# A fused attention, linear-attention and mixture-of-experts kernel: one written-out order for every engine, and a first block table after five of eight images

## What is computed

```python
# 1. attention inside each image, with a key mask, added to x
sim = softmax(q.T @ k / sqrt(64) + key_mask);  x = x + gamma * (sim @ v)
# 2. on tokens t (8 images x 256 pixels, 128 channels), with LayerNorm: causal
#    linear attention of 8 heads over the IMAGE axis: image i sums over images 0..i
t = t + linear_attention(layer_norm(t)) @ out_w.T + out_b
# 3. with LayerNorm: 8 experts, the top 2 of each token, weights normalised
h = silu(x @ w1[e]) * (x @ w3[e]);  t = t + sum over the 2 chosen e of weight * (h @ w2[e])
```

## Time and profile before

| | |
|---|---|
| time, median of 3 runs (lowest to highest) | 201.02 us (199.63 to 201.24) |
| profiled execution, its own time | 201.14 us |
| its span, first to last instruction | 199.3 us |
| PE busy, share of the span | 147.9 us, 74% |
| DVE, POOL, ACT busy | 126.2, 88.2, 73.5 us |
| DMA moved | 16.91 MB |

### The profile page before, as it was taken

One profiled execution on the slowest core, in us unless ns is written; L12 is line 12 of the kernel. 1 busy time (PEld: TensorE's weight loads), 2 busy tenths in 40 slices (PEclk: granted clock), 3 DMA queues, 4 the chain that ended last, 5 costly groups with the idle time before them and its releaser, 6 DMA issues.

```text
span 199.3 us, 4128 instructions
## 1 busy us (share of the span) xinstructions
PE 147.9 (74%) x1125; PEld 129.2 (65%) x1125; DVE 126.2 (63%) x464; ACT 73.5 (37%) x222; POOL 88.2 (44%) x94
## 2 busy tenths in 40 slices
PE   0879999999979589684943057999999999992000
PEld 0557788798767457383823045999999999991000
DVE  2526776799989595997365500667767676752263
ACT  2357686667362204221114001444444444440000
POOL 0001111022023718087787750278787878776000
PEclk9999999999999967996555555999999999999555
DMA  5889600000000101011111714223243333110595
GB/s 131 228 265 363 247 3 0 0 3 0 0 5 13 40 0 56 1 43 42 40 57 53 153 48 105 62 79 92 76 100 84 92 92 85 47 53 0 178 251 204
DMA packets 15476, 16.91 MB, mean 85 GB/s; under 512 B 3083, under 2 KB 14032, under 8 KB 15198
## 3 DMA queue, kind: packets, MB, share of 16 engines
q1 hardware_dynamic: 12606, 12.14, 20.8%
q0 software_dynamic: 2272, 4.24, 6.8%
q10 hardware_dynamic: 576, 0.27, 0.8%
HBM read 10.76 MB, written 6.33 MB: 86 GB/s over the span
## 4 chain that ended last, share of the span: by engine, by line
PE 54%; issue 11%; DVE 11%; DMA 8%; POOL 7%; SPq 3%; ACT 3%; POOLq 0%; DVEq 0%; ACTq 0%
PE ps L759 18%; PE ps L768 8%; POOL rows_x L449 4%; PE ps L610 3%; DMA y<-rows_y 3%; PE ps L630 3%; PE ps L750 2%; PE ps L669 2%; PE ps L690 2%; PE ps L595 2%; DVE num L920 2%; DMA XT<-in_x_tok 2%; PE ps L596 2%; PE ps L620 2%; DVE xrow L952 2%
## 5 line engine op out<-in xcount | busy, mean ns | idle before, releaser
L461 POOL DMA_INDIRECT rows_y<-yb,xb x39 | 43.9, 1124 | 21.9 <-DVE yb L1068 21.0
L759 PE MATMUL ps<-xbT,WB 128*128 128x128 f32 x312 | 42.7, 282 | 0.0
L449 POOL DMA_INDIRECT rows_x<-xrow,slot x32 | 32.3, 1008 | 22.8 <-DVE slot L1013 14.2
L759 PEld LDWEIGHTS ps<-xbT,WB 128*128 128x128 f32 x312 | 39.4, 198 | 0.1
L433 POOL TENSOR_TENSOR rs<-ve,CF 128x2 f32<-128x2 f32 x8 | 5.6, 702 | 42.9 <-DVE ve L863 42.9
L1068 DVE TENSOR_SCALAR yb<-ps,xb 128x128 f32<-128x128 f32 x39 | 13.7, 351 | 17.2 <-PE ps L768 17.2
L572 ACT ACTIVATE gate<-ps 128x256 f32<-128x256 f32 x39 | 14.9, 383 | 25.6 <-PE ps L759 25.6
L768 PE MATMUL ps<-W,hid 128*128 x156 | 23.7, 276 | 0.5 <-DVE hid L1051 0.5
L1051 DVE TENSOR_TENSOR hid<-gate,ps 128x256 f32<-128x256 f32 x39 | 16.0, 411 | 11.0 <-ACT gate L572 11.0
L768 PEld LDWEIGHTS ps<-W,hid 128*128 128x128 f32 x156 | 20.5, 192 | 0.7 <-issue 0.7
L566 ACT ACTIVATE xbT<-ps 128x128 f32<-128x128 f32 x39 | 10.8, 277 | 19.3 <-PE ps L750 19.3
(11 more groups left out here) (126 smaller groups left out, 281.2 us busy)
## 6 DMA issues: line engine op xcount, KB each, us to landing
xb<-rows_x SPq DMA_DIRECT2D x39, 65.0 KB, 2.0
W<-in_w SPq DMA_DIRECT2D x1, 2048.0 KB, 10.3
y<-rows_y SPq DMA_DIRECT2D x8, 192.0 KB, 4.8
X<-in_x_ch SPq DMA_DIRECT2D x8, 128.0 KB, 2.9
XT<-in_x_tok SPq DMA_DIRECT2D x8, 128.0 KB, 3.4
W<-in_w SPq DMA_DIRECT2D x1, 1024.0 KB, 12.4
out_tok<-y SPq DMA_DIRECT2D x4, 192.0 KB, 3.6
rows_y<-yb,xb POOLq DMA_INDIRECT x39, 2.4
```

Source lines behind the costliest of these rows:

```text
L449: pool.indirect_dma_start(rows_x, bass.IndirectOffsetOnAxis(ap=slot[:, g:g + 1], axis=0), xrow[:, i * T + t, c, :], None, bounds_check=DUM ...
L461: pool.indirect_dma_start(rows_y, bass.IndirectOffsetOnAxis(ap=xb[:, n, DEST_COL:ROW].bitcast(I32), axis=0), yb[:, n, :], None, bounds_che ...
L759: last = pe.matmul(ps_gu[s % 3][:, k * P:(k + 1) * P], WB[:, s % WBS, k * P:(k + 1) * P], xbT[:, s % XBT, :], start=True, stop=True)
```

## The change

The steps and lags go. Each engine's list is written out call by call, and so is the PSUM bank of every call (thirteen tables of numbers; any of the eight banks can serve any purpose). In the written lists, stages one and two overlap:

- **Two tables.** `TABLES` holds (images counted, blocks, first block). After five images a first table hands out 13 blocks, only whole ones of 128 rows (the count is rounded down); after eight a second one hands out the other 26, starting where the first left off (`table_taken`), rounded up.
- **The first 13 blocks' w1 and w3** come from DRAM by a DMA on SP each (`load_weights`, 256 KB); the other 26 are copied by DVE as before.
- **Normalisations on ACT.** `lin_norm` and `route_norm` become activations with scale and bias. POOL prepares them: the eps addition comes from DVE, and -mean and -mean*rstd are new, so `rstd_lin` and `rstd_ffn` are four POOL instructions in place of one, with two waits on POOL's own semaphore.
- **Weighting on ACT**: `weigh` is an activation with a per-row scale. The silu table is loaded in mid-stage (`silu_set`).
- The 16 extra matmuls ahead of stage two (`WARM_MATMULS`) go. All eight pads are issued by SP, and five constants by ACT's queue. The first image's x and its token copy have semaphores of their own. y1 and y2 reuse the space of XT and X. Buffers grow: XBT, GATE, HID, WBS from 4, 3, 4, 3 to 6, 4, 5, 5.

```diff
-XBT, GATE, HID, WBS = 4, 3, 4, 3
-BANKS_XBT, BANKS_GU, BANKS_YB = (0, 1), (3, 4, 6), (2, 5)
+XBT, GATE, HID, WBS = 6, 4, 5, 5
+TABLES = ((5, 13, 0), (8, 26, 13),)
+BANK_CQK = (1, 3, 5, 0, 7, 2, 2, 6)
...
-WARM_MATMULS = 16
-STEPS = B + 12
...
             def rstd_ffn(i):
-                pool.wait_ge(ve2_done, i + 1)
+                b = i % 2
+                pool.wait_ge(mv2_done, 2 * (i + 1))
                 if i >= 2:
                     pool.wait_ge(xrow_done, 2 * (i - 1))
-                pool.tensor_tensor(rs2[:, i % 2, :], ve2[:, i % 2, :], CF[:, C_HALF:C_HALF + T], ALU.pow).then_inc(rs2_done, 1)
+                pool.tensor_scalar(nm2[:, b, :], mv2[:, b, :, 0], -1.0, None, ALU.mult)
+                link(pool.tensor_scalar(ve2[:, b, :], mv2[:, b, :, 1], LN_EPS, None, ALU.add))
+                link(pool.tensor_tensor(rs2[:, b, :], ve2[:, b, :], CF[:, C_HALF:C_HALF + T], ALU.pow))
+                pool.tensor_tensor(nb2[:, b, :], nm2[:, b, :], rs2[:, b, :], ALU.mult).then_inc(rs2_done, 1)
...
+            def route_norm(i):
+                b = i % 2
+                act.wait_ge(rs2_done, i + 1)
+                for t in range(T):
+                    act.activation(xrow[:, i * T + t, :, 0:P], t2[:, i * T + t, :].unsqueeze(1).broadcast_to([P, TOP_K, P]),
+                                   ACT.Identity, bias=nb2[:, b, t:t + 1], scale=rs2[:, b, t:t + 1]).then_inc(xrow_done, 1)
...
+            for k, (_, blocks, first) in enumerate(TABLES):
+                if k == len(TABLES) - 1:
+                    pad_lists()
+                sp.wait_ge(table_done, k + 1)
+                for n in range(k + 1):
+                    images = TABLES[n][0] - (TABLES[n - 1][0] if n else 0)
+                    sp.wait_ge(scattered[n], 16 * images * T * TOP_K)
+                if k == len(TABLES) - 1:
+                    sp.wait_ge(pads_stored, 16 * (E + 1))
+                for s in range(first, first + blocks):
+                    load_rows(s)
+                    if k < len(TABLES) - 1:
+                        load_weights(s)
...
+            def weigh(s):
+                n = s % RING
+                act.wait_ge(yb_done_pe, s + 1)
+                if s >= RING:
+                    act.wait_ge(yb_stored[n], 16 * (s // RING))
+                act.activation(yb[:, n, :], bank(BANK_YB[s])[:, 0:P], ACT.Copy, scale=xb[:, n, W_COL:W_COL + 1]).then_inc(yb_done, 1)
...
+            rstd_lin(0); rstd_lin(1); rstd_lin(2); rstd_lin(3); rstd_ffn(0); rstd_lin(4); rstd_ffn(1)
+            scatter(0, 0); scatter(0, 1); scatter(0, 2); scatter(0, 3); rstd_lin(5); rstd_ffn(2); scatter(1, 0)
...
```

More of the change, by code:

```diff
@@ L68 @@
 T_ROW, T_EXPERT = range(2)
+NO_EXPERT = 1 << 14
 def constants():
@@ L322, in hybrid_block @@
         wb_done = sem("wb_done")
+        wb_loaded = [sem(f"wb_loaded{n}") for n in range(WBS)]
         yb_done_pe = sem("yb_done_pe")
@@ L341, in pieces, with table_of @@
             return sum(len(halves(i)) for i in range(n))
[L343 to L355, removed]
+        def table_of(s):
+            return [k for k, (_, _, first) in enumerate(TABLES) if first <= s][-1]
         def table_reader(eng, line, most):
             sets = [[eng.alloc_register(f"line{line}_{half}_{n}") for n in range(READ)] for half in range(2)]
+            turn = [1]
             def read(s):
[L362 to L366, removed]
+                _, blocks, first = TABLES[table_of(s)]
+                n = (s - first) % READ
+                if n == 0:
+                    turn[0] = 1 - turn[0]
+                    m = min(READ, first + blocks - s)
+                    eng.reg_load(sets[turn[0]][0:m], table[line:line + 1, s:s + m])
+                return eng.snap(sets[turn[0]][n], min_val=0, max_val=most)
             return read
@@ L668, in lin_scores @@
                     strip = STRIP * (j - first)
-                    last = pe.matmul(ps_hs[strip:strip + STRIP, share, :], heads, qk[:, i % 2, j, :], start=True, stop=True)
+                    last = pe.matmul(two(BANK_HS[i])[strip:strip + STRIP, share, :], heads, qk[:, i % 2, j, :],
+                                     start=True, stop=True)
                 if end == i + 1:
@@ L732, in route_rank @@
                           start=False, stop=True).then_inc(rank_done, 1)
-            for step in range(STEPS):
-                run_step(step, (lin_scores_turn, 5), (lin_proj_qk, 4), (lin_proj_v, 5), (route_rank, 9), (conv_proj_v, 1), (lin_out_turn, 6),
-                         (conv_turn, 2), (conv_scores, 1), (route_logits, 8), (lin_out, 6), (lin_turn, 3), (conv_out, 2),
-                         (lin_scores, 4, 0), (conv_proj_qk, 0), (lin_scores, 4, 1), (route_turn, 7))
-            pe.wait_ge(seen_done, B + 1)
@@ L770, in down @@
                 last.then_inc(yb_done_pe, 1)
[L772 to L789 removed]
+            conv_proj_v(0); conv_proj_qk(0); conv_scores(0); conv_proj_qk(1); conv_proj_v(1); conv_proj_qk(2)
```

682 lines of the change are left out of this document (407 added, 275 removed).

## The result

The changed kernel takes 203.67 us, median of 4 runs (202.98 to 204.96), beside 201.13 (199.63 to 201.58) for the kernel before on the same chip: a ratio of 1.020, 95% interval 1.013 to 1.027. It is about 2% slower. The profiled execution of the changed kernel took 204.96, its span 202.7; its last result starts at 186.3, 31.4 us later than the 154.9 of the sum.

The account below looks back on a forecast made before the run. POOL's list was taken as the bound, PE nearly tied: first scatter 45.5, first five images' rows out 81.5, last scatters done 106.6, plus 48.3 of results to 154.9, 16.6 to the end and 1.84 outside: 173.3 us, range 165 to 187.

Parts of the forecast that it names:

- First scatter: POOL's first scatter, 62.78 us before, was to start at 45.5 us, after a rank done at 45.1.
- POOL up to the first table: POOL's 20 scatters of images 0 to 4 (26.2 us) plus seven normalisation groups of 1.4 (9.8), ending at 81.5 us.
- The first table to the last scatter: Chain through four engines from 81.5 us: first `gate_up` 89.3, image 7's transpose 93.5, table chain 101.4, four scatters until 106.6.
- A: Interval from the first normalised row to the last scatter's start; 84.0 us by the forecast's sum.
- The near tie of PE and POOL: Second table's blocks: PE reaches the last at 152.8 us, result a little later; POOL is later by about 1.7.
- C: Interval from the start of block 13's result to the last result, 25 blocks; 34.1 us by the forecast's sum.
- Another read, issue and landing: Second table's start: after pads landing at 111.2 us, SP's register read, issue and row landing (1.45 + 0.48 + 2.0) give 115.1.
- B: Interval from the last scatter's start to the start of block 13's result; 15.5 us by the forecast's sum.
- Normalisations: nothing on the chain.: Normalisations and weightings moved to ACT at 0.383 and 0.277 us each, 21 us in all, within ACT's idle time.
- 3: Rival, 20%: waits in the written order hold each list, groups cost 2.0 us; 11.7 us more, 185 in all.
- 2: Rival, 15%: DVE holds POOL's DMAs; 24 scatters on the path cost 5.0 us more, 178.3 in all.
- 4: Rival, 3%: PE stays at half clock through the second table, 2.9 us a block instead of 1.45; 201 to 209 us.

Follow-up runs that it names:

- kernel 13: Changed kernel with one edit: VectorE copies the first 13 blocks' weights too, SP only asks for their rows; 197.15 us, ratio 0.980.
- kernel 7: Changed kernel with SP issuing the eight pads behind the weights of block 9 instead of block 12; 203.03 us, ratio 1.012.
- 10: Changed kernel with POOL's second new order, register reads one block ahead and regular order for blocks 13 to 38; 195.57 us, ratio 0.968.
- kernel 12: Like 10, but one table for all 39 blocks behind the last image, regular order, all weights copied by VectorE; 198.22 us, ratio 0.984.
- kernel 5: Changed kernel with only POOL's calls reordered, five normalisation groups ahead of the scatters they stood behind; 200.05 us, ratio 0.995.
- 2: Changed kernel with VectorE's two attention products each replaced by two multiplications with a constant; 198.59 us, ratio 0.984.
- 3: Changed kernel with PE and ACT in the regular order of before for blocks 13 to 38; 200.70 us, ratio 1.004.
- kernel 4: Changed kernel with registers read from the block tables one block ahead on PE, VectorE and SP; 198.20 us, no ratio given.
- kernel 11: Like 10, with the first 13 blocks' weights copied by VectorE instead of 256 KB transfers on SP; 188.26 us, ratio 0.933.
- 1: Changed kernel with both normalisations and the epsilon back on VectorE, one power per normalisation on POOL; 211.58 us, ratio 1.066.
- 6: Changed kernel with normalisations back on VectorE and POOL's new order of kernel 5; 205.74 us, ratio 1.026.

## Why the prediction was wrong, step by step

- **First scatter.** 45.5 forecast, 48.12 measured. PE's first matmul came at 4.37, 1.4 earlier than before, where 1.9 was forecast; but its pairs of matmuls then took 1.06 us until 12.6, where before they took 0.60 from 10.01 on. The rank ended at 46.0 instead of 45.1, and the scatter followed 2.1 later instead of 0.4. In kernel 13, which has the same lists up to there, the pairs take 0.60 from 8.93 on and the first scatter comes at 45.63; in kernel 7 it comes at 45.77. These two met the forecast, but by two misses that cancel: a rank 1.6 early and the 2.1 behind it. The granted clock from 10 to 12 us is 1.00 in all four, so what sets the pace of the start is open. The changed kernel and kernel 13:
```profile
10.05 1.06 PE L707 MATMUL ps<-X,WC 128*65 128x256 f32 x2
```
```profile
8.93 0.60 PE L705 MATMUL ps<-X,WC 128*65 128x256 f32 x2
...
45.63 2.15 POOL L500 DMA_INDIRECT rows_x<-xrow,slot  x1 [2.12 <-DVE slot L1129]
```
- **"POOL up to the first table"** is the step that failed most: 36.0 forecast, 49.0 measured (48.12 to 97.13). The 20 scatters were busy for 24.4 us, 4.3 more than at 1.008 each, and 8.3 of idle time stood before them instead of 6.0. The seven groups lasted 13.3, that is 1.90 each and not 1.4 (1.60 where nothing held them, 55.22 to 56.82). And POOL stood 3.0 ahead of groups, 2.55 of it for one image's mean from DVE, where the sum had nothing. So 7.8 of the 13.0 are POOL's own items, priced too low; the rest, some 5 us, is idle time, most of it waiting for images that the sum took as ready whenever POOL was. From 48 to 98 us ten of POOL's instructions took 0.15 us or more over their time alone, and each of the ten ran beside a product of `lin_products` or `lin_values` on DVE, like this one of 0.23 alone:
```profile
75.48 1.16 POOL L476 TENSOR_SCALAR nm<-mv 128x2 f32<-128x2 f32 x1
```
```profile
75.33 1.23 DVE L1053 TENSOR_TENSOR num<-vt,sco 128x1024 f32<-128x1024 f32 x1
```
- **"The first table to the last scatter."** The first `gate_up` came 10.6 us behind the end of image 4's scatters (97.13 to 107.71), 7.8 were forecast. The last scatter was seen as landed 3.0 after POOL's instruction had ended, where 1.5 was taken. PE's list has three transposes ahead of the first `gate_up`, so it waited for the rows of block 2, asked for at 103.81, where the sum had asked only for those of block 0; they took 3.3 to land instead of 2.0. The three `gate_up` took 4.9 instead of 4.2, the way from image 7's transpose to the end of the table chain 6.4 instead of 7.7, and image 7's first scatter followed 1.2 later instead of 0.2: 120.27 for 101.4, where 2.6 + 13.0 + 2.8 + 0.7 - 1.3 + 1.0 are the 18.9.
```profile
96.15 3.96 DMA rows_x<-xrow,slot
...
103.81 3.32 DMA xb<-rows_x
...
107.71 1.72 PE ps L879 x8
```
- **What the runs say of A.** Of its 18.8 us, 3.6 are the groups behind scatters (changed against 10; 3.7 against 5), 6.0 the early blocks (10 against 12), and 9.2 remain even with one table and POOL's new order (93.2 against 84.0). DVE's products have a part in these: without them, in the old order, A is 3.2 shorter (2). The rest no run splits. Counted from the first normalised row, image 7's transpose came at 86.0 before, at 82.3 in kernel 12 and at 91.3 in the changed kernel; the sum had 72.2. Nothing in the change made the images come that much earlier, and the earlier trace rows had the transpose at 103.82.
- **The near tie of PE and POOL in C** was no tie. POOL waits for ACT's weighting 23.1 us in all; the 1.27 for the last nine results needed PE to be done early. Of the 8.1 us, the written order is 4.6 (3), reads are 0.8 (4), and the remaining 2.7 were not tested by themselves; the kernel before already had 35.7 there and kernel 12 has 35.8, 1.6 above the 34.1 of the sum.
- **"Another read, issue and landing"** had the right terms: pads, read of 1.45 (1.71), rows. It even had the weight transfers' wait for PE ahead of the pads, but put its end at 102.3 and took it to be hidden; SP issued the pads from 124.21 on, though their row numbers were there at 116.8, and with that wait gone B is 14.4 (11).
- **"Normalisations: nothing on the chain."** ACT takes 0.593 and 0.486 us, not 0.383 and 0.277. The rows that were taken as a match have no operand per partition; for 128x256, `qT` with one (a bias column) takes 0.466, and these normalisations have two, scale and bias. That the columns alone make the difference was not tested. Still a gain (1, 6).
- **Rivals.** 3 named part of what happened, waits in the written order and groups of 2.0 (1.90 measured), and priced it at 11.7 instead of 31. 2 was right in kind, and more than priced on POOL: 4.3 in the 20 scatters up to the first table and 2.2 in the seven groups (13.3 - 7 x 1.59), beside 5.0 for all 24 scatters. 4 did not happen: after 120 us only two `gate_up`, between 138 and 143, ran at half clock (1.91 each; granted 0.50 from 138 to 142), after PE's 4.5 us of waiting. The Trainium skill, "GPSIMD Engine Reference", section 8, names two SBUF inputs of VectorE, or its use of both ports, as the cause of contention: the 2.16 beside a product agrees. The 1.73 stood beside one-input multiplications, so two inputs are not needed; whether those use both ports no row here shows.

A check that would have caught it: by the earlier trace rows, image 7 was transposed at 103.82 before, and routing, scatters and the table took until the first `gate_up` at 122.50 from there. Even with PE's 26 blocks at 1.45 right behind it and the tail of 16.6 that is 176.8, not 171.5, unless the change brings image 7 earlier or shortens that way; kernel 11 reaches a span of 187.1.

## What to carry to other kernels

When work moves under an earlier stage, first ask when that stage's last input is ready in the old trace; a list of one engine gives a bound only between such points. On an in-order queue, look for what a short, ready item stands behind: the pads behind weight waits cost 7 us, the powers behind scatters 2.5%. The powers were one reordering away; moving the pads forward alone gained nothing (7), the waits had to leave that queue (11). Order written out by hand should keep a distance of a block or two between the links of a chain; batches of three left gate, silu, hidden and down exposed.

## What the runs showed of the hardware

- An indirect DMA of POOL, 0.97 us alone, took 2.16 beside a VectorE product of 1.22 and 1.73 beside two one-input multiplications of 0.69 us from SBUF to SBUF; POOL's power of 0.71 took 1.69 beside such a product (kernel 5).
- A register read from the block table took 0.5 to 1.7 us on SP, and left PE idle for 1.53 where it stood in front of a matmul; one block ahead it cost PE 0.8 once, while VectorE's read of 1.45 still stood ahead of a product (kernel 4).
- An ACT normalisation with scale and bias per partition took 0.593 us for 128x256 and 0.486 for 128x128, slower than VectorE's 0.412 for the former; ACT took 0.466 for 128x256 with a bias column alone and 0.384 with none.
